# Attention and expert kernel: projection pieces cut in halves, one inverse square root for two norms, a new order of writes on the SyncE queue

## The chip, the cores and the metric

The kernel runs on one core of one Trainium2 chip. A core has TensorE (matrix products), VectorE, ScalarE, GpSimd, and SyncE, which here only issues DMAs. The metric is device microseconds of one execution. Everything that is not an output lives in on-chip SBUF, in the PSUM banks that TensorE writes, or in scratch tensors in DRAM.

## The reference

x and ctx are (8, 256, 512): batch, channel or row, time. Without the set-up code the reference is:

```
ln(x)   = (x - mean) / sqrt(var + 1e-5)               # over the last axis
q, k, v = Wq ln(x) + bq, Wk ctx + bk, Wv ctx + bv     # 1x1 projections, 256 channels
p       = softmax(q^T k / 4) per head                 # 16 heads of 16 channels, 512 x 512 scores
x1      = x + Wo (p v) + bo
z       = ln(x1)
h       = z * rsqrt(mean(z * z) + 1e-6) * rms_weight
top 2 of 8 experts by h router_w; moe = sum of weight * (silu(h Wg_e) * (h Wu_e)) Wd_e
out     = x1 + moe + (silu(h Sg) * (h Su)) Sd
```

All in float32. The second norm is a layer norm followed at once by an RMS norm of the same rows.

## The kernel before

The attention runs in 16 **slots** s = 0 to 15 (HALVES), one for half the heads of one batch: slot s works on batch s // 2. A slot has 32 **units** u, one for a tile of 128 keys by 512 queries of one head. The loop on each engine walks u in steps of two (ScalarE in steps of one) in program order, so the order is written out by hand, and semaphores join the engines.

TensorE does in each step of two units (loop at L903): the scores of both units (L850, into three PSUM banks st_ps), the max-pass products of two units of a later slot (L816, into three banks front_ps; the pass runs up to two slots ahead), and in every second step the products of four probability tiles with V (L863). ScalarE turns scores into probabilities (L725). VectorE reduces the max pass to row maxima (L963). When a slot's maxima are complete, TensorE turns them (turn_max, L835, at unit 12), VectorE copies them into a high and a low part (max_parts, L971 and L973, at unit 14), SyncE writes them out as rows (rows_out, L511) and reads them back under the Q stack (rows_in, L519), where the next slot's scores need them.

Between these, **projection pieces** run in one PSUM bank, proj_ps, which is handed from piece to piece. Slot s projects K and Q for slot s + 3, K at unit 2 and Q at unit 6 (KQ_UNITS, L246; project_qk, L779). At units 18 and 26 (late_units, L254) an even slot projects V for the next batch (project_v, L803), an odd slot the output projection of batch (s - 3) / 2 (project_out, L345). A piece is six matmuls of 512 columns or twelve of 256, since each product is made as high x high + high x low + low x high. ScalarE empties K and Q with their bias (qk_bias, L678) and V (v_copy) two units after the piece; VectorE adds the output projection to x (residual, L415, two units after) and takes its row statistics (L1006, four units after).

GpSimd has one list per slot (L633): the high and low part of K (L580, L584), the same of Q; in even slots then the load of C two batches ahead (L641), normalize (L594), the split of x (L600, L602) and the split of C (L614, L616); in odd slots split_attn (L607, L609), the split of the attention output for the output projection; then in both the division by the softmax sums (L410). project_out waits for split_attn by the semaphore attn_split, at its first matmul. In split_attn:

```
pool.wait_ge(attn_ready, ATTN_START + 2 * (b + 1))
pool.wait_ge(low_ready, 2 * min(2 * b + 7, HALVES))
```

SyncE's queue (L537) does per slot, in this order: numerators and denominators of the slot before out and back in, K parts out (write_part, L490), the K stack in (load_stack, L504), Q parts out, the maxima's rows out, the inverted denominators out (rec_out), the rows in, the inverted denominators in (rec_in), the Q stack in.

The norms need 1 / sqrt on VectorE without ScalarE's tables: a bit trick and three Newton steps, eleven small chained operations (row_rstd). row_scale does it twice, once for the layer norm and once for the RMS norm: in slot 14 for batches 0 to 5 (in three lumps at units 0, 4 and 8), and after the attention for batch 6 and for batch 7. In slot 3 one chain at unit 16 makes the input norm of batches 4 to 7. After the attention come the shared expert, the routing and 39 blocks of 128 rows through the experts; the change does not touch them.

Of the kernel before, what the change touches and what calls it, by code (L numbers as in the profile page):

```python
# [53 lines left out]
def xattn_ffn_kernel(nc, x, ctxt, wqkv_t, wo_t, bias_cols, rms_w, router_t, gate_up, down,  # L54
# [15 lines left out]
    with ExitStack() as outer:  # L70
# [15 lines left out]
        rstd2 = sb("rstd2", [P, B * CT])  # L86
# [103 lines left out]
        var_ready = sem("var_ready")  # L190
# [98 lines left out]
        count = {"step": 0, "var": 0}  # L289
# [75 lines left out]
        def row_variance(dve, lo, hi):  # L365
# [5 lines left out]
        def row_rstd(dve, lo, hi, dst, done=None):  # L371

            count["var"] += 1
            dve.wait_ge(var_ready, count["var"])
# [3 lines left out]
                                                 ALU.mult, ALU.add))  # L378
            for i in range(NEWTON):
                chained(dve, nc.vector.tensor_tensor(rs_c[:, lo:hi], rs_b[:, lo:hi], rs_b[:, lo:hi], ALU.mult))  # L380
                chained(dve, nc.vector.scalar_tensor_tensor(out=rs_c[:, lo:hi], in0=rs_c[:, lo:hi], scalar=-0.5, in1=rs_a[:, lo:hi],
                                                            op0=ALU.mult, op1=ALU.mult))
                last = nc.vector.scalar_tensor_tensor(out=(rs_b if i < NEWTON - 1 else dst)[:, lo:hi], in0=rs_c[:, lo:hi], scalar=1.5,
                                                      in1=rs_b[:, lo:hi], op0=ALU.add, op1=ALU.mult)
                if i < NEWTON - 1 or done is None:
                    chained(dve, last)
                else:
                    last.then_inc(done, 1)

        def row_scale(dve, lo, hi, steps=(0, 1, 2)):  # L390
            if 0 in steps:
                row_variance(dve, lo, hi)
            if 1 in steps:
                row_rstd(dve, lo, hi, rstd)
                chained(dve, nc.vector.tensor_tensor(rs_a[:, lo:hi], mv[:, lo:hi, 1], rstd[:, lo:hi], ALU.mult))
                chained(dve, nc.vector.tensor_tensor(rs_a[:, lo:hi], rs_a[:, lo:hi], rstd[:, lo:hi], ALU.mult))
                nc.vector.tensor_scalar(rs_a[:, lo:hi], rs_a[:, lo:hi], RMS_EPS, None, ALU.add).then_inc(var_ready, 1)
            if 2 in steps:
                row_rstd(dve, lo, hi, rstd2)
                chained(dve, nc.vector.tensor_tensor(rstd[:, lo:hi], rstd[:, lo:hi], rstd2[:, lo:hi], ALU.mult))  # L400
# [71 lines left out]
        with nc.Block() as block:  # L472

            @block.sync
            def _(sp):
# [61 lines left out]
                for s in range(HALVES):  # L537
# [26 lines left out]
            def _(pool):  # L564
# [68 lines left out]
                for s in range(HALVES):  # L633
                    if s + 3 < HALVES:
# [3 lines left out]
                    b = (s + 4) // 2  # L638
                    if s % 2 == 0 and b < B:
                        pool.wait_ge(v_ready, 2 * (b - 1))  # L640
                        nc.gpsimd.dma_start(c_sb[:, b % 2, :, :], c_t[b]).then_inc(c_loaded[b % 2], 16)  # L641
                        normalize(b)
                        split_xn(b)
                        split_c(b)
# [26 lines left out]
            def _(act):  # L671
# [46 lines left out]
                for s in range(HALVES):  # L718
                    proj = s + 3 < HALVES
                    for u in range(UNITS):  # L720
# [10 lines left out]
                        if proj and u - 2 in KQ_UNITS:  # L731
                            qk_bias(s + 3, KQ_UNITS.index(u - 2))
                        if value_batch(s) is not None and u - 2 in late_units(s):
                            v_copy(value_batch(s), late_units(s).index(u - 2))
# [3 lines left out]
            def _(pe):  # L738
# [9 lines left out]
                def project_qk(n, i, kts=range(CT)):  # L748
# [35 lines left out]
                def project_v(b, r):  # L784

                    if r == 1:
                        pe.wait_ge(vt_copied, 2 * b + 1)
                    elif b < 2:
                        pe.wait_ge(qk32_ready, 4 * (b + 1))
                    else:  # L790
                        pe.wait_ge(nm_parts_ready, turns(2 * b - 1))
                    for i in range(2):
# [12 lines left out]
                    mm.then_inc(v_ready, 1)  # L805
# [850 lines left out]
```

## Time and profile before

| | |
|---|---|
| median of 3 runs | 850.28 us (850.21 to 852.99) |
| profiled execution | 849.69 us, its span 847.9 us |
| TensorE busy | 803.9 us, 95% |
| VectorE busy | 518.1 us, 61% |
| ScalarE busy | 401.1 us, 47% |
| GpSimd busy | 353.1 us, 42% |
| attention slots | from about 54 to 516 us |

Busy time is what an engine's instructions cover. Matmuls overlap in the pipeline and their ends are modelled, so a TensorE shown as busy may still wait for a moment; start to start is the better measure of a matmul. A timeline row gives the start, the length, the engine and line, and in square brackets the idle time before it and what ended it.

### The profile page before, as it was taken

The page shows a single profiled execution, that of the slowest core. Times are in us where ns is not written, and L with a number is a line of the kernel's source. Part 1 is how long each engine was busy: PE and PEld are TensorE (multiplying, and loading weights), DVE is VectorE, ACT ScalarE, POOL GpSimd, SP SyncE. Part 2 cuts the span into 40 slices and gives each one's busy share as a digit, 9 for nine tenths or more (in the row PEclk, how much of TensorE's full clock was granted, in tenths as well). Part 3 has the DMA queues.
Part 4 walks back from the last instruction along what each step waited for, and adds up shares of the span by engine and source line. Part 5 has one row for each costly group of instructions (what it writes and reads, how often), then busy time and mean ns, then how long its engine had stood idle before and what let it go on. Part 6 is the DMA issues. An engine that isn't in the chain of part 4 may idle for free. (4 is left out here: it accounts for less than half of the span.)

```text
span 847.9 us, 11463 instructions
## 1 busy us (share of the span) xinstructions
PE 803.9 (95%) x3771; PEld 388.6 (46%) x3771; DVE 518.1 (61%) x1043; ACT 401.1 (47%) x751; POOL 353.1 (42%) x288
## 2 busy tenths in 40 slices
PE   6999999999999999999999998999999999999993
PEld 2434434444444444444433454443555555555552
DVE  5787888787777877878788655568542222222221
ACT  1115666767677677676776663110422323333231
POOL 4207417326354274253220211000117777777774
PEclk9999999999999999999999999999999999999998
DMA  8957557646665566466633223931626555655553
GB/s 275 211 95 224 114 127 166 132 103 141 145 137 129 119 157 149 103 149 143 131 80 106 91 77 110 415 111 51 251 56 99 98 97 97 101 90 96 95 98 43
DMA packets 54956, 110.48 MB, mean 130 GB/s; under 512 B 12580, under 2 KB 27684, under 8 KB 50660
## 3 DMA queue, kind: packets, MB, share of 16 engines
q1 hardware_dynamic: 37852, 80.23, 37.5%
q0 software_dynamic: 16960, 29.37, 18.4%
q8 instruction: 32, 0.52, 0.3%
q10 hardware_dynamic: 88, 0.16, 0.1%
q14 instruction: 24, 0.20, 0.1%
HBM read 68.44 MB, written 41.16 MB: 129 GB/s over the span
## 5 line engine op out<-in xcount | busy, mean ns | idle before, releaser
L963 DVE TENSOR_REDUCE negmax<-front_ps 128x1 f32<-128x512 f32 x512 | 323.6, 681 | 85.9 <-PE front_ps L816 85.5
L725 ACT ACTIVATE probs<-st_ps 128x512 f32<-128x512 f32 x512 | 280.2, 601 | 166.6 <-PE st_ps L850 149.9
L1215 POOL DMA_INDIRECT out<-x_sb,row_i x78 | 122.0, 1564 | 70.3 <-ACT x_sb L1263 57.0
L1408 PE MATMUL big_ps<-w_gu,attn 128*128 x312 | 140.4, 593 | 0.8 <-ACT attn L1255 0.8
L1602 DVE TENSOR_TENSOR zeros<-attn,big_ps 128x256 f32<-128x256 f32 x39 | 16.4, 421 | 116.3 <-ACT attn L1275 116.3
L850 PE MATMUL st_ps<-stacks 50*128 50x512 f32 x256 | 77.7, 488 | 5.4 <-ACT probs L725 4.3
L1408 PEld LDWEIGHTS big_ps<-w_gu,attn 128*128 128x128 f32 x312 | 56.2, 190 | 57.0 <-issue 57.0
L410 POOL TENSOR_TENSOR attn<-attn,recip 128x512 f32<-128x512 f32 x15 | 19.2, 1278 | 150.1 <-DMA recip<-rec_dram 150.1
L850 PE MATMUL st_ps<-q_stack,k_stack 50*128 50x512 f32 x256 | 74.6, 491 | 3.9 <-ACT probs L725 2.8
L580 POOL CAST early<-early 128x512 fp32r<-128x512 f32 x28 | 17.1, 610 | 136.4 <-ACT early L678 136.4
L816 PE MATMUL front_ps<-stacks 48*128 48x512 f32 x256 | 68.7, 434 | 3.8 <-DVE negmax L963 3.0
L1275 ACT ACTIVATE attn<-big_ps 128x256 f32<-128x256 f32 x39 | 15.0, 384 | 117.7 <-PE big_ps L1408 117.7
L816 PE MATMUL front_ps<-k_stack,q_stack 48*128 48x512 f32 x256 | 69.2, 425 | 0.8 <-DVE negmax L963 0.3
L863 PE MATMUL pv_ps<-probs,v_t 128*32 128x512 f32 x512 | 68.2, 605 | 0.5 <-ACT probs L725 0.5
L863 PE MATMUL pv_ps<-probs,early 128*32 128x512 f32 x512 | 68.2, 605 | 0.3
L850 PEld LDWEIGHTS st_ps<-stacks 50*128 50x128 f32 x256 | 29.6, 183 | 82.8 <-ACT probs L725 71.4
L1199 POOL DMA_INDIRECT x_sb<-h_rows,row_i x39 | 39.5, 1013 | 61.0 <-DVE row_i L1576 49.4
L850 PEld LDWEIGHTS st_ps<-q_stack,k_stack 50*128 50x128 f32 x256 | 28.4, 183 | 77.0 <-ACT probs L725 67.0
L1377 PE MATMUL big_ps<-down_high,act_parts 128*128 x156 | 59.1, 419 | 1.1 <-DVE act_parts L1594 1.1
L1291 PE MATMUL big_ps<-early,sh_gu 128*128 128x512 f32 x128 | 56.3, 594 | 0.0
L584 POOL TENSOR_TENSOR early<-early 128x512 fp32r<-128x512 f32 x32 | 41.0, 1281 | 12.3 <-DVE early L955 10.0
L1592 DVE CAST act_parts<-big_ps 128x256 fp32r<-128x256 f32 x39 | 16.5, 424 | 46.7 <-PE big_ps L1386 46.7
(199 smaller groups left out, 1056.6 us busy)
## 6 DMA issues: line engine op xcount, KB each, us to landing
parts_dram<-early SPq DMA_DIRECT2D x32, 512.0 KB, 6.2
stacks<-parts_dram SPq DMA_DIRECT2D x32, 256.0 KB, 5.6
w_gu<-in_gate_up SPq DMA_DIRECT2D x8, 1024.0 KB, 13.4
x_sb<-in_x SPq DMA_DIRECT2D x8, 512.0 KB, 9.9
early<-in_ctx POOLq DMA_DIRECT2D x8, 512.0 KB, 7.1
stacks<-parts_dram SPq DMA_DIRECT2D x32, 128.0 KB, 5.9
k_stack<-parts_dram SPq DMA_DIRECT2D x16, 256.0 KB, 5.1
q_stack<-parts_dram SPq DMA_DIRECT2D x16, 256.0 KB, 5.6
```

The costliest lines, as they stand in the source:

```text
L410: eng.tensor_tensor(half, half, recip[:, :], ALU.mult).then_inc(attn_ready, 1)
L584: nc.gpsimd.tensor_tensor(parts[:, i, 1, :], qk32[:, i, :], parts[:, i, 0, :].bitcast(F32), ALU.subtract).then_inc(low_ready, 1)
L725: nc.scalar.activation(probs[:, k % 2, u % GH, :], score_bank(UNITS * s + u), ACT.Exp, scale=SCALE).then_inc(exp_done, 1)
L816: nc.tensor.matmul(smax_bank(i), q_stack[buf][low:low + SROWS, pair, tt * P:(tt + 1) * P], k_stack[buf][low:low + SROWS, pair, :], start=T ...
L850: nc.tensor.matmul(score_bank(i), k_stack[buf][low:end, pair, st * P:(st + 1) * P], q_stack[buf][low:end, pair, :], start=True, stop=True, ...
L863: mm = nc.tensor.matmul(pv_ps[32 * j:32 * j + 32, :], v_t[n % NBUF][:, st, GH * g + j, :], probs[:, k % 2, j, :], start=(st == 0), stop=(s ...
L963: nc.vector.tensor_reduce(negmax[:, n % 2, c:c + 1], smax_bank(UNITS * n + u), AX_X, ALU.max, negate=True).then_inc(max_done, 1)
L1199: nc.gpsimd.indirect_dma_start(h_in[:, k % RING, :], None, h_rows, bass.IndirectOffsetOnAxis(ap=row_i[:, k:k + 1], axis=0)).then_inc(in_lo ...
L1215: nc.gpsimd.indirect_dma_start(outs[i], bass.IndirectOffsetOnAxis(ap=row_i[:, k:k + 1], axis=0), y_sb[:, k % RING, DY * i:DY * (i + 1)], N ...
L1291: mm = nc.tensor.matmul(big_ps[:, 2 * (j % 2) + i, :], sh_gu[:, a, i * F + c * P:i * F + (c + 1) * P], ht_all[:, g, a, :], start=(a == 0), ...
L1377: mm = nc.tensor.matmul(y_ps[:, k % 2, :], act[:, a, :], w[:, bass.ds(expert, 1), a, :], start=(a == 0 and i == 0), stop=(a == FT - 1 and ...
L1408: mm = nc.tensor.matmul(gu_ps[:, :], h_t[:, k % 2, a, :], w_gu[:, bass.ds(expert, 1), a, :], start=(a == 0), stop=(a == DT - 1))
```

## The change

In slots 3 to 12 (`spread`) each projection piece is done in two halves of three matmuls (V: six) four units apart: K at units 2 and 6, Q at 10 and 14, V or output at 18 and 22, and 26 and 30. A piece is emptied two units after its second half, that is K at unit 8, Q at 16, the third at 24, the fourth at unit 0 of the next slot. The turn of the maxima moves from unit 12 to unit 8, its copies from unit 14 to unit 8. VectorE takes the row statistics directly behind the residual. On SyncE the K stack's load moves behind the rows out, and the Q parts' write behind the rows in. On GpSimd the load of C moves to the head of the list and the split of C before the normalization, in all even slots. The norm after the attention becomes one inverse square root of var * (1 + 1e-6) + 1e-11, which is the product of the two; its steps in slot 14, and those of slot 3, are spread over units. project_out also waits for qk32_ready.

The core of the diff (left out: the count of the variance semaphore, renamed callers, the unchanged bodies of the Newton steps):

```diff
-        KQ_UNITS = (2, 6)
+        def spread(s):
+            return 3 <= s < HALVES - 3
         def turn_unit(s):
-            return 16 if s == 0 else 12
+            return 16 if s == 0 else 8 if spread(s) else 12
+        def parts_unit(s):
+            return turn_unit(s) if spread(s) else turn_unit(s) + 2
+        def kq_units(s):
+            return ((2, 6), (10, 14)) if spread(s) else ((2, 2), (6, 6))
         def late_units(s):
-            return (10, 14) if s == 0 else (18, 26)
+            return ((18, 22), (26, 30)) if spread(s) else ((10, 10), (14, 14)) if s == 0 else ((18, 18), (26, 26))
+        def halves_at(pieces, u):
+            for i, units in enumerate(pieces):
+                if u in units:
+                    return i, [j for j, unit in enumerate(units) if unit == u]
+            return None, []
+        def ended_at(pieces, u):
+            ends = [units[1] for units in pieces]
+            return ends.index(u - 2) if u - 2 in ends else None
...
         def project_out(pe, b, o, kt, bank):
                 pe.wait_ge(nm_parts_ready, turns(min(2 * b + 4, HALVES - 1)))
+                pe.wait_ge(qk32_ready, 2 * min(2 * b + 7, HALVES))
...
-            nc.vector.tensor_scalar(rs_a[:, lo:hi], mv[:, lo:hi, 1], LN_EPS, None, ALU.add).then_inc(var_ready, 1)
+            chained(dve, nc.vector.tensor_scalar(rs_a[:, lo:hi], mv[:, lo:hi, 1], scale, eps, ALU.mult, ALU.add))
-        def row_scale(dve, lo, hi, steps=(0, 1, 2)):
...
+        def token_variance(dve, lo, hi):
+            row_variance(dve, lo, hi, 1.0 + RMS_EPS, LN_EPS * RMS_EPS)
+        def token_scale(dve, lo, hi):
+            token_variance(dve, lo, hi)
+            row_rstd(dve, lo, hi)
...  SyncE
                     if proj:
                         write_part(s + 3, 0)
-                        load_stack(s + 3, 0)
-                        write_part(s + 3, 1)
+                        if not spread(s):
+                            load_stack(s + 3, 0)
+                            write_part(s + 3, 1)
                     if s + 1 < HALVES:
                         rows_out(s + 1)
+                    if proj and spread(s):
+                        load_stack(s + 3, 0)
                     if s > 0:
                         rec_out(sp, s - 1)
                     if s + 1 < HALVES:
                         rows_in(s + 1)
+                    if proj and spread(s):
+                        write_part(s + 3, 1)
                     if s > 0:
                         rec_in(sp, s - 1)
...  GpSimd
+                    b = (s + 4) // 2
+                    if s % 2 == 0 and b < B:
+                        pool.wait_ge(v_ready, 2 * (b - 1))
+                        nc.gpsimd.dma_start(c_sb[:, b % 2, :, :], c_t[b]).then_inc(c_loaded[b % 2], 16)
                     if s + 3 < HALVES:
                         for i in range(2):
                             high(s + 3, i)
                             low(s + 3, i)
                     if s % 2 == 0 and b < B:
+                        split_c(b)
                         normalize(b)
                         split_xn(b)
-                        split_c(b)
...  TensorE
                     elif 0 in kts:
                         pe.wait_ge(xn_ready, n // 2 + 1)
+                        if spread(s):
+                            pe.wait_ge(nm_parts_ready, turns(s + 1))
                 def turn_max(n):
-                    pe.wait_ge(qk32_ready, 2 * min(n + 3, HALVES))
+                    pe.wait_ge(qk32_ready, min(2 * n + 5, 2 * HALVES) if spread(n - 1) else 2 * min(n + 3, HALVES))
...
-                        if out_batch(s) is not None and u in late_units(s):
-                            for kt in range(CT):
-                                project_out(pe, out_batch(s), late_units(s).index(u), kt, proj_ps[:, :])
+                        if out_batch(s) is not None:
+                            for kt in parts_here:
+                                project_out(pe, out_batch(s), i, kt, proj_ps[:, :])
...  VectorE
                         if s == 3 and u == 16:
-                            row_rstd(dve, 4 * CT, B * CT, rstd, scale_ready)
+                            rstd_guess(dve, 4 * CT, B * CT)
+                        if s == 3 and u in (20, 22, 24):
+                            rstd_step(dve, 4 * CT, B * CT, (u - 20) // 2, scale_ready if u == 24 else None)
+                        if u == 0 and spread(s - 1) and out_batch(s - 1) is not None:
+                            residual(dve, out_batch(s - 1), 1, proj_ps[:, :])
+                            row_stats_of(out_batch(s - 1), 1)
-                        if u == turn_unit(s) + 2 and s + 1 < HALVES:
+                        if u == parts_unit(s) and s + 1 < HALVES:
                             max_parts(s + 2, UNITS)
...
-                            row_scale(dve, 0, EARLY, (u // 4,))
+                            token_variance(dve, 0, EARLY)
+                        if s == HALVES - 2 and u == 2:
+                            rstd_guess(dve, 0, EARLY)
+                        if s == HALVES - 2 and u in (4, 6, 8):
+                            rstd_step(dve, 0, EARLY, (u - 4) // 2)
...
-                row_scale(dve, EARLY, LAST)
+                token_scale(dve, EARLY, LAST)
```

## Rows read from the trace of the kernel before

**Rows 1.** Page, parts 1, 2, 5: busy us (share) xcount; tenths; busy, mean ns | idle.
```profile
PE 803.9 (95%) x3771; PEld 388.6 (46%) x3771; DVE 518.1 (61%) x1043; ACT 401.1 (47%) x751; POOL 353.1 (42%) x288
...
PEclk9999999999999999999999999999999999999998
...
L963 DVE TENSOR_REDUCE negmax<-front_ps 128x1 f32<-128x512 f32 x512 | 323.6, 681 | 85.9 <-PE front_ps L816 85.5
```

**Rows 2.** TensorE's timeline, slots 3 to 5: start us, length us, line, out<-in, count [idle before].
```profile
152.04 0.50 PE L779 MATMUL proj_ps<-c_high,w_high 128*128 128x512 f32 x1
...
182.06 0.50 PE L779 MATMUL proj_ps<-c_high,w_high 128*128 128x512 f32 x1
...
183.64 0.50 PE L850 MATMUL st_ps<-stacks 50*128 50x512 f32 x2
183.98 0.40 PE L816 MATMUL front_ps<-stacks 48*128 48x512 f32 x2
184.31 1.07 PE L863 MATMUL pv_ps<-probs,early 128*32 128x512 f32 x8
185.31 0.50 PE L850 MATMUL st_ps<-stacks 50*128 50x512 f32 x2
...
185.97 0.50 PE L779 MATMUL proj_ps<-xn_high,w_high 128*128 128x512 f32 x1
186.31 0.40 PE L779 MATMUL proj_ps<-down_high,w_high 128*128 128x512 f32 x1
186.54 0.39 PE L779 MATMUL proj_ps<-xn_high,w_low 128*128 128x512 f32 x1
...
187.56 0.50 PE L850 MATMUL st_ps<-stacks 50*128 50x512 f32 x2
...
188.22 1.06 PE L863 MATMUL pv_ps<-probs,early 128*32 128x512 f32 x8
...
191.16 1.06 PE L863 MATMUL pv_ps<-probs,early 128*32 128x512 f32 x8
...
209.75 0.50 PE L779 MATMUL proj_ps<-c_high,w_high 128*128 128x512 f32 x1
```

**Rows 3.** ScalarE's timeline: the Q bias in slots 4 and 5.
```profile
188.58 0.68 ACT L678 ACTIVATE early<-proj_ps,bias 128x512 f32<-128x512 f32 x1
...
216.27 0.68 ACT L678 ACTIVATE early<-proj_ps,bias 128x512 f32<-128x512 f32 x1
```

**Rows 4.** VectorE's timeline, slot 5: residual and row statistics.
```profile
227.27 0.74 DVE L415 SCALAR_TENSOR_TENSOR x_sb<-proj_ps,bo_all,x_sb 128x512 f32<-128x512 f32 x1
...
229.12 0.68 DVE L1006 BATCH_NORM_STATS2 stats<-x_sb 128x6 f32<-128x512 f32 x1
```

**Rows 5.** TensorE's timeline: output projection of slot 5, K piece of slot 6.
```profile
223.70 0.50 PE L345 MATMUL proj_ps<-down_high,w_o_high 128*128 128x512 f32 x1
...
238.06 0.50 PE L779 MATMUL proj_ps<-c_high,w_high 128*128 128x512 f32 x1
```

**Rows 6.** GpSimd's timeline, slot 5: second instruction of the attention split.
```profile
220.23 2.38 POOL L609 TENSOR_TENSOR attn_low<-attn,down_high 128x1024 fp32r<-128x1024 f32 x1
```

**Rows 7.** TensorE's timeline, slot 3, beside VectorE's square-root chain.
```profile
169.62 0.50 PE L816 MATMUL front_ps<-stacks 48*128 48x512 f32 x1 [0.53 <-DVE negmax L963]
```

**Rows 8.** SyncE's queue, slot 4: last issue of the Q stack.
```profile
205.30 0.42 SPq L506 DMA_DIRECT2D q_stack<-parts_dram  x1
```

**Rows 9.** TensorE's timeline, slot 14.
```profile
471.23 1.10 PE L746 MATMUL proj_ps<-zeros 128*128 128x512 f32 x2 [0.79 <-DVE nm_parts L973]
```

**Rows 10.** Timeline after the attention: VectorE's last step for batch 7, TensorE's turn.
```profile
546.09 0.16 DVE L400 TENSOR_TENSOR rstd<-rstd 128x2 f32<-128x2 f32 x1
...
548.79 0.44 PE L444 MATMUL front_ps<-ident,rows_or_down 128*128 128x128 f32 x2 [0.53 <-DVE rows_or_down L427]
```

**Rows 11.** TensorE's last matmul, and a stretch: busy us of each engine, PEclk, DMA.
```profile
835.31 0.40 PE L1377 MATMUL big_ps<-down_high,act_parts 128*128 x1
...
840.00:841.00 1.00, 0.00 (x0) 0.00 (x0) 0.00 (x0) 0.00 (x0) 0.70 (x2) 0.87 0.00 0
```

More of the change, by code:

```diff
@@ L288, in xattn_ffn_kernel @@
         EARLY = LAST - CT
-        count = {"step": 0, "var": 0}
+        count = {"step": 0}
         def out_batch(s):
@@ L378, in row_rstd @@
                                                  ALU.mult, ALU.add))
-            for i in range(NEWTON):
[L380 to L388, printed above, removed]
@@ L390, in row_scale, with rstd_step @@
-        def row_scale(dve, lo, hi, steps=(0, 1, 2)):
[L391 to L400, printed above, removed]
+        def rstd_step(dve, lo, hi, i, done=None):
+            chained(dve, nc.vector.tensor_tensor(rs_c[:, lo:hi], rs_b[:, lo:hi], rs_b[:, lo:hi], ALU.mult))
+            chained(dve, nc.vector.scalar_tensor_tensor(out=rs_c[:, lo:hi], in0=rs_c[:, lo:hi], scalar=-0.5, in1=rs_a[:, lo:hi],
+                                                        op0=ALU.mult, op1=ALU.mult))
+            last = nc.vector.scalar_tensor_tensor(out=(rs_b if i < NEWTON - 1 else rstd)[:, lo:hi], in0=rs_c[:, lo:hi], scalar=1.5,
+                                                  in1=rs_b[:, lo:hi], op0=ALU.add, op1=ALU.mult)
+            if done is None:
+                chained(dve, last)
+            else:
+                last.then_inc(done, 1)
@@ L730, in _ @@
                             pv_copy(2 * s)
[L731 to L734, printed above, removed]
+                        if u == 0 and spread(s - 1) and value_batch(s - 1) is not None:
+                            v_copy(value_batch(s - 1), 1)
+                        if proj and ended_at(kq_units(s), u) is not None:
+                            qk_bias(s + 3, ended_at(kq_units(s), u))
+                        if value_batch(s) is not None and ended_at(late_units(s), u) is not None:
+                            v_copy(value_batch(s), ended_at(late_units(s), u))
                 pv_copy(2 * HALVES - 1)
@@ L782, in project_qk, with project_v @@
                         mm.then_inc(qk_ready, 1)
[L784 to L792, printed above, removed]
+                def project_v(b, r, tiles=(0, 1)):
+                    if 0 in tiles:
+                        if r == 1:
+                            pe.wait_ge(vt_copied, 2 * b + 1)
+                        else:
+                            pe.wait_ge(qk32_ready, 4 * (b + 1))
+                            if b >= 2:
+                                pe.wait_ge(nm_parts_ready, turns(2 * b - 1))
+                    for i in tiles:
                         st = 2 * r + i
@@ L804, in project_v @@
                                                           start=(kt == 0 and j == 0), stop=(kt == CT - 1 and j == PRODUCTS - 1))
-                    mm.then_inc(v_ready, 1)
+                    if 1 in tiles:
+                        mm.then_inc(v_ready, 1)
                 def max_pass(n, u):
@@ L911, in _ @@
                             pv(STEPS * s + u // GH - 1)
-                        if s + 3 < HALVES and u in KQ_UNITS:
-                            project_qk(s + 3, KQ_UNITS.index(u))
+                        i, kts = halves_at(kq_units(s), u)
+                        if s + 3 < HALVES and kts:
+                            project_qk(s + 3, i, kts)
                         if u == turn_unit(s) and s + 1 < HALVES:
                             turn_max(s + 1)
-                        if value_batch(s) is not None and u in late_units(s):
-                            project_v(value_batch(s), late_units(s).index(u))
-                        if out_batch(s) is not None and u in late_units(s):
-                            for kt in range(CT):
-                                project_out(pe, out_batch(s), late_units(s).index(u), kt, proj_ps[:, :])
+                        i, parts_here = halves_at(late_units(s), u)
+                        if value_batch(s) is not None and parts_here:
+                            project_v(value_batch(s), i, parts_here)
+                        if out_batch(s) is not None:
+                            for kt in parts_here:
+                                project_out(pe, out_batch(s), i, kt, proj_ps[:, :])
                         if s == 0 and u == 0:
```

29 lines of the change are left out of this document (12 added, 17 removed).

## The prediction

> **What bounds the kernel now.** I read the page first. TensorE is busy for 95% of the span, at the full granted clock of 2.4 GHz [rows 1], so a gain must come out of TensorE's own sequence and not out of another engine's load. "Busy" hides short waits, because the ends of matmuls are modelled, so the second view is TensorE's timeline of slot 4. Its steps are regular [rows 2]: a pair of score matmuls 0.34 us (183.64 to 183.98), a pair of max-pass matmuls 0.33, the eight products with V 1.00 (184.31 to 185.31). A group of four units from one V product to the next is V product, scores, maxima, piece, scores, maxima. With a six-matmul projection piece it takes 188.22 - 184.31 = 3.91 us, without one 191.16 - 188.22 = 2.94 us. The work of the second is only 1.00 + 2 x (0.34 + 0.33) = 2.34 us, so 0.60 us of each group without a piece is spent on the round trip through VectorE's maxima and ScalarE's exponentials. Slot 4 has four groups of each sort: 4 x (3.91 + 2.94) = 27.4, and the turn of the maxima adds 0.2. The K pieces of slots 4 and 5 start 27.69 us apart (182.06, 209.75) [rows 2], which agrees.
>
> **Halves in slots 3 to 12: the gain.** The piece takes 1.59 us (185.97 to 187.56). Its first matmul costs 0.34, the next 0.23 each, the last 0.33 with the change back to the scores [rows 2]. Half a piece, three matmuls, is 0.34 + 0.23 + 0.33 = 0.90. Every group of four units now holds one half: 3.91 - (1.59 - 0.90) = 3.22 us, above the 2.94 of the round trip, so that wait vanishes behind real work. Two groups take 6.44 instead of 6.85: 0.41 saved per piece, four pieces a slot, **1.6 us**. Bounds: at least 0.8, if a switch to a half piece and back costs twice what I read (0.2 more per piece); at most 4 x (6.85 - 2 x 2.94) = 3.9, if half a piece vanished wholly in the round trip's 0.60. I take 1.6, which is the reading itself, for K, Q, V and output pieces alike, since each is six matmuls of 512 columns or twelve of 256.
>
> Against it stand tighter hand-overs. The turn now follows the V product of unit 8 directly. The K bias on ScalarE starts 1.02 us after the scores of its unit (187.56 to 188.58) and takes 0.68 [rows 2, 3]; TensorE wants the bank at 0.34 + 0.33 + 1.00 = 1.67, so it waits about 0.1. The two copies of the turned maxima must then end before the Q piece of unit 10: another 0.1. So a slot without an output piece goes from 27.7 to 27.7 - 1.6 + 0.2 = 26.3 us: **-1.4**, five times (slots 4, 6, 8, 10, 12): -7.0.
>
> In odd slots VectorE's residual (0.74 us) and row statistics (0.68) [rows 4] now stand one behind the other, and the next piece reuses the bank only two units later. The pair's maxima end about 2.05 us after its scores (0.34, 0.40 for the first product, two reductions of 0.68 that overlap a little [rows 1]), the residual at 2.75; TensorE is there at 2.34: 0.45 us of wait, twice per odd slot. Odd slots show 238.06 - 209.75 = 28.31 us now [rows 2, 5]; without what follows they would be 26.3 + 0.9 = 27.2: -1.1. Bounds of the 0.9: from 0.6, what they lose to the same work now (28.3 - 27.7), to 1.5.
>
> **The wait that the change creates.** GpSimd runs its list in order. In an odd slot it is: high and low part of K, high and low part of Q, then the split of the attention output into its high and low part, then the division. That order is not edited. But the bias of Q, on which the Q parts wait, moves from unit 8 to unit 16, and the output projection, which needs the split (attn_split), stays at unit 18. Now: Q's bias starts at 216.27 [rows 3], the second instruction of the split starts at 220.23 and lasts 2.38 [rows 6], so the split is there 222.61 - 216.27 = 6.34 us after the bias started. The projection starts at 223.70 [rows 5], 1.1 us after that: no wait today. After the change the bias starts 1.02 us after the scores of unit 16, the split is ready at 1.02 + 6.34 + 0.06 = 7.4 us, and TensorE stands at the projection after 0.34 + 0.33 + 1.00 + 0.34 + 0.33 = 2.34 us. **It waits 5.1 us**, in slots 3, 5, 7, 9 and 11. Behind the waiting matmul are all later scores, maxima and V products; ScalarE and VectorE run empty, and nothing gives the time back, since every group after it is bound by TensorE. Bounds: not under 3.5 (if ScalarE's bias came 1.6 us ahead of its place, which in-order exponentials exclude), not above 7 (if GpSimd's steps stretched by a third). An odd slot then takes 27.2 + 5.1 = 32.3 instead of 28.3: **+4.0**, four times (5, 7, 9, 11): +16.0. Slot 3 takes 182.06 - 152.04 = 30.02 us now, since eleven chained square-root steps on VectorE make TensorE wait there, 0.53 us in one row [rows 2, 7]; spread out they cost some 0.2, so slot 3 comes to 32.5: +2.5.
>
> **Other edges.** In even slots GpSimd gets Q at about 15 us, splits C until 20.8, normalizes, splits x until 28.5, 2 us into the next slot; the first user, Q's piece at unit 10, comes 8 us into it, C's at unit 2: nothing lost. On SP the Q parts are written only after the maxima's rows; each queue step behind them counts. Today the last load of the Q stack is issued at 205.30 [rows 8], 25.6 us after the slot's first scores (2.3 before 182.06), and its first user is unit 8 of the next slot, 35.6 us after them. In the new order the bias of Q is done at 15 us, its parts at 17, SP writes them at 18.3 once the maxima's rows are through, waits for the inverted rows until about 22.5 and issues the last load near 24.5; the user comes at 26.3 + 6.8 = 33.1. So 8.6 us of cover where there are 10.0 today. I cost it at nothing; if the landing takes longer, slots 5, 7, 9 and 11 pay what is missing, up to 2 us each. C's load moves to the head of GpSimd's list, away from the stack loads, and is used 15 us later: nothing. The new wait for qk32_ready in the output projection is met whenever attn_split is: nothing.
>
> One inverse square root for both norms: in slot 14 TensorE's 0.79 us wait for the copies of the maxima [rows 9] goes, since VectorE no longer runs a second chain of twelve steps ahead of them: -0.8 (0 to -1.5). For batch 6 at the end of attention, VectorE waits for the denominators' DMA anyway: nothing. For batch 7 the chain ends in 546.09 + 0.16 today; fifteen steps of 0.2 go [rows 10], and TensorE's wait of 0.53 before the turn at 548.79 [rows 10] vanishes, the rest being under its own gates: -0.5 (0 to -3).
>
> **The sum.** -7.0 + 16.0 + 2.5 - 0.8 - 0.5 = +10.2 on the profiled execution of 849.69 us (span 847.9 and 1.8 around it): 859.9. The median of the three runs stands 0.6 higher at 850.28, so 860.5 us.
>
> **Rivals.**
> *The clock falls in the new waits.* TensorE stands still for 5.0 us each time. At the end of this trace its last matmul ends at 835.7 and the granted clock of 840 to 841 us is 0.87, of which 0.26 us at the half level: it fell 5.0 us after the last matmul [rows 11], from 2.4 to 1.2 GHz. For it: the same length of rest. Against it: gaps up to 2.1 us in this trace left it at 1.00. If it falls, the matmuls behind each wait run at half speed for a while; between half a group (+1.6 us) and a whole one (+3.2): +8 to +16, so 868.5 to 876.5, nearer the first.
> The Trainium skill, "TensorE: Matmul & The Clock Gate", Part 1, says that the clock is halved after the array has been idle and given back only after it has been busy again for some time; by that rule this rival is the forecast, by the forecast's sum it is not; the row at the end of the trace agrees with the rule and can't tell whether 5.0 us are enough in mid-kernel.
>
> *The stacks come late.* The Q stack of the next slot lands after unit 8 of odd slots: +1 to +2 in four slots, 864.5 to 868.5. For it: the cover shrinks by 1.4 us. Against it: odd slots are longer by the wait itself.
>
> *No wait at unit 18: faster.* If the split is done before TensorE reaches unit 18, the gains stand alone: five even slots -7.0, four odd -4.4, slot 3 at 27.4 instead of 30.0 -2.6, -1.3 elsewhere: -15.3, so 835 us. It would take a TensorE that arrives later (bound by VectorE or ScalarE) or a split that runs ahead of Q's parts. The break is at a wait of 15.3 / 5 = 3.1 us instead of 5.1: below it the change is no loss. For it: the halves fill idle time as computed. Against it: GpSimd's order and four measured durations.
>
> **Numbers.** Forecast 0.62 (own range 855 to 865), clock 0.18, stacks 0.06, faster 0.14 (0.01 of it so near to nothing that it counts as no change). About 0.5% is what a measurement of this kernel tells from no change. Slower by over 0.5%: 0.83; within: 0.04; faster: 0.13. The range 853 to 874 leaves out the faster case and the far end of the clock's.
>
> **What would show it.** Odd slots of 32 us and even ones of 26.3; in TensorE's waits five of about 5 us at the output projection, released by GpSimd's second split instruction; no wait there in even slots; groups of 3.22 us without the 2.94 ones; granted clock below 1 behind the waits only if the first rival holds. If the five waits are absent the forecast is wrong by its main step and the time is near 835; if they are there but the slots between are not shorter, the halves' step failed.

## The result, and the profile after

Over six runs each the changed kernel takes 884.44 us (879.41 to 886.27) and the kernel before 850.50 (849.69 to 852.99): ratio 1.038, 95% interval 1.036 to 1.040. The forecast was 860.5 with a range from 853 to 874: slower as forecast, but by 34 us and not by 10. The profiled run took 884.68 us, its span is 882.9, 35.0 more than before.

The same parts of the page after (busy us, share, xcount; tenths of the clock; busy, mean ns | idle):

```profile
PE 812.1 (92%) x3771; PEld 380.8 (43%) x3771; DVE 519.6 (59%) x998; ACT 405.2 (46%) x751; POOL 353.0 (40%) x288
...
PEclk9999999899799899899699999999999999999998
...
L1001 DVE TENSOR_REDUCE negmax<-front_ps 128x1 f32<-128x512 f32 x512 | 326.7, 685 | 111.9 <-PE front_ps L852 110.1
```

Beside [rows 1] the number of matmuls is the same and TensorE's busy time is 8.2 us longer. The clock's line says why: it was 9 in every slice but the last, and now has dips from slice 8 to slice 20, which is the attention. VectorE's maxima are as long as before.

The waits of TensorE after (who waited on whom: us in total, times, longest; some rows left out):

```profile
PE proj_ps L367 <- POOL attn_low L638: 25.2, 5, 5.1
PE front_ps L852 <- DVE negmax L1001: 4.0, 7, 0.8
PE proj_ps L813 <- DVE x_sb L439: 3.4, 5, 0.7
...
PE proj_ps L813 <- DVE nm_parts L1011: 2.1, 10, 0.2
PE proj_ps L367 <- DVE x_sb L439: 1.9, 3, 1.2
```

The first is the forecast wait: five times 5.1 us (4.93 in slot 3, 5.06 in the others) at the output projection, released by the second split instruction. The rows on x_sb (at the K piece) and on nm_parts are hand-overs that the forecast put at 0.45 and 0.1 us each: 0.7 and 0.2.

One odd slot (11) after. TensorE's timeline, which answers to [rows 5]:

```profile
374.56 0.47 PE L813 MATMUL proj_ps<-c_high,w_high 128*128 128x512 f32 x1 [0.68 <-DVE x_sb L439]
...
400.96 0.50 PE L813 MATMUL proj_ps<-c_high,w_high 128*128 128x512 f32 x1
...
414.10 0.40 PE L852 MATMUL front_ps<-stacks 48*128 48x512 f32 x2
419.56 0.77 PE L367 MATMUL proj_ps<-down_high,w_o_high 128*128 128x512 f32 x1 [5.06 <-POOL attn_low L638]
420.13 0.63 PE L367 MATMUL proj_ps<-attn_low,w_o_high 128*128 128x512 f32 x1
420.55 0.63 PE L367 MATMUL proj_ps<-down_high,w_o_low 128*128 128x512 f32 x1
421.12 0.80 PE L886 MATMUL st_ps<-q_stack,k_stack 50*128 50x512 f32 x2
421.71 0.63 PE L852 MATMUL front_ps<-stacks 48*128 48x512 f32 x2
422.27 1.93 PE L899 MATMUL pv_ps<-probs,v_t 128*32 128x512 f32 x8
424.13 0.79 PE L886 MATMUL st_ps<-q_stack,k_stack 50*128 50x512 f32 x2
...
437.38 1.07 PE L899 MATMUL pv_ps<-probs,v_t 128*32 128x512 f32 x8
...
439.82 0.47 PE L813 MATMUL proj_ps<-c_high,w_high 128*128 128x512 f32 x1 [0.71 <-DVE x_sb L439]
```

ScalarE's Q bias and GpSimd's list in the same slot (answering to [rows 3] and [rows 6]):

```profile
413.12 0.68 ACT L708 ACTIVATE early<-proj_ps,bias 128x512 f32<-128x512 f32 x1
```

```profile
413.87 0.61 POOL L609 CAST early<-early 128x512 fp32r<-128x512 f32 x1 [5.05 <-ACT early L708]
414.56 1.27 POOL L613 TENSOR_TENSOR early<-early 128x512 fp32r<-128x512 f32 x1
415.96 1.04 POOL L636 CAST down_high<-attn 128x1024 fp32r<-128x1024 f32 x1
417.08 2.34 POOL L638 TENSOR_TENSOR attn_low<-attn,down_high 128x1024 fp32r<-128x1024 f32 x1
```

And the same stretch cut into windows (us, busy us and count of PE, PEld, DVE, ACT, POOL, granted clock as a share of 2.4 GHz, DMA share, GB/s):

```profile
414.50:417.00 2.50, 0.00 (x1) 0.00 (x0) 1.29 (x2) 1.37 (x3) 2.30 (x2) 1.00 0.97 153
417.00:419.50 2.50, 0.00 (x0) 0.00 (x0) 0.00 (x0) 0.00 (x0) 2.34 (x1) 0.61 0.87 222
419.50:434.00 14.50, 14.44 (x49) 5.61 (x53) 6.65 (x11) 4.91 (x10) 1.27 (x1) 0.50 0.42 73
434.00:439.00 5.00, 5.00 (x31) 1.54 (x23) 3.96 (x7) 2.78 (x7) 0.00 (x0) 0.94 0.00 0
```

Q's bias starts at 413.12. The split is ready at 417.08 + 2.34 = 419.42, 6.30 us later (forecast 6.34). GpSimd's first instruction, Q's high part, had itself waited 5.05 us for that bias. Before the wait is over, at about 417.6, the clock falls from 2.4 to 1.2 GHz. It stays at 1.2 through 14.5 us in which TensorE is busy for 14.44, and comes back at about 435. Eight products with V take 422.27 to 424.13 = 1.86 us where they took 1.00 [rows 2]. So this odd slot lasts 439.82 - 400.96 = 38.86 us instead of 28.3. The even one ahead of it lasts 400.96 - 374.56 = 26.40, where 27.69 stood before and 26.3 was forecast.

I read the clock in 1-us windows over the whole span. Before it never left 1.00 in the attention. After, it is at 1.2 GHz there in seven stretches, 54.6 us in all: one at each of the five waits (6.8, 10.2, 6.8, 6.8 and 17.1 us long), one at 182 to 186, and one at 485 to 490 (3.4 us each), the last in slot 13, where there is no long rest. Each of the five begins inside its wait, 2.9 to 4.4 us after TensorE stopped. So the forecast wait is there, and a cost that the sum did not have lies on top.

### The profile page after: what moved, and what is told of

Read it like the earlier page. It is cut to its first block and busy times, and to the rows that moved or that the text cites. A ratio compares the mean times of both kernels' runs of the same rounds, so it can differ in the third digit from the quotient of the medians.

```text
span 882.9 us, 11450 instructions
## 1 busy us (share of the span) xinstructions
PE 812.1 (92%) x3771; PEld 380.8 (43%) x3771; DVE 519.6 (59%) x998; ACT 405.2 (46%) x751; POOL 353.0 (40%) x288
## 5 line engine op out<-in xcount | busy, mean ns | idle before, releaser
L755 ACT ACTIVATE probs<-st_ps 128x512 f32<-128x512 f32 x512 | 284.3, 598 | 197.0 <-PE st_ps L886 180.3
L609 POOL CAST early<-early 128x512 fp32r<-128x512 f32 x28 | 17.1, 611 | 227.0 <-ACT early L708 227.0
L899 PE MATMUL pv_ps<-probs,v_t 128*32 128x512 f32 x512 | 72.7, 642 | 0.5 <-ACT probs L755 0.5
L886 PE MATMUL st_ps<-stacks 50*128 50x512 f32 x256 | 69.8, 504 | 2.2 <-ACT probs L755 2.0
L899 PE MATMUL pv_ps<-probs,early 128*32 128x512 f32 x512 | 70.4, 623 | 0.3 <-ACT probs L755 0.2
L886 PE MATMUL st_ps<-q_stack,k_stack 50*128 50x512 f32 x256 | 68.9, 516 | 0.8 <-ACT probs L755 0.7
L852 PE MATMUL front_ps<-stacks 48*128 48x512 f32 x256 | 59.6, 430 | 2.9 <-DVE negmax L1001 2.2
L852 PE MATMUL front_ps<-k_stack,q_stack 48*128 48x512 f32 x256 | 60.2, 417 | 2.1 <-DVE negmax L1001 1.8
L886 PEld LDWEIGHTS st_ps<-stacks 50*128 50x128 f32 x256 | 26.3, 187 | 77.7 <-ACT probs L755 61.6
L886 PEld LDWEIGHTS st_ps<-q_stack,k_stack 50*128 50x128 f32 x256 | 25.8, 190 | 75.4 <-ACT probs L755 58.3
```

The lines of the kernel that those rows point to most:

```text
L755: nc.scalar.activation(probs[:, k % 2, u % GH, :], score_bank(UNITS * s + u), ACT.Exp, scale=SCALE).then_inc(exp_done, 1)
L852: nc.tensor.matmul(smax_bank(i), q_stack[buf][low:low + SROWS, pair, tt * P:(tt + 1) * P], k_stack[buf][low:low + SROWS, pair, :], start=T ...
L886: nc.tensor.matmul(score_bank(i), k_stack[buf][low:end, pair, st * P:(st + 1) * P], q_stack[buf][low:end, pair, :], start=True, stop=True, ...
L899: mm = nc.tensor.matmul(pv_ps[32 * j:32 * j + 32, :], v_t[n % NBUF][:, st, GH * g + j, :], probs[:, k % 2, j, :], start=(st == 0), stop=(s ...
```

## The experiments

The theory after the result (A): the 35.0 us are the wait (25.2), the clock behind it (about 18), and a gain of the halves that is smaller than forecast (about -8 instead of -15). Rivals: that the clock costs little and the halves themselves cost time; that the clock falls whatever the length of the rest; that the new order of SyncE's queue holds the stacks back.

### The split ahead of Q's parts

attn_high shares its memory with qk32, the tile into which the projected K and Q are emptied (both start at element 3072 of the same buffer). That is why the split waits for Q's low part, the last reader of qk32; a change of order alone would overwrite K and Q. Here it has 4 KB per partition of its own, shared in time with data that is reloaded in slot 14, and the split heads GpSimd's list:

```
+ attn_high = sb("attn_high", [P, 2, T], F32R)
...
- pool.wait_ge(low_ready, 2 * min(2 * b + 7, HALVES))
+ pool.wait_ge(bo_ready, 1)
+ pool.wait_ge(wo_split, 1)
+ if b > 0: pool.wait_ge(y_ready, CT * b)
...
  for s in range(HALVES):
+     if out_batch(s) is not None and out_batch(s) < B - 2:
+         split_attn(out_batch(s))
      if s + 3 < HALVES: ...
-     (the same two lines behind Q's and K's parts)
```

> The changed kernel with its split of the attention output moved from behind Q's high and low part to the head of GpSimd's list in odd slots. For that the split's high half gets a place of its own (that of w_o and rms_w, which are loaded again in slot 14), since its old place is the one of the K and Q tile. Theory (the wait at unit 18 and the clock that falls behind it are the whole loss): the five waits of 5.1 us go, the granted clock stays at 1.00 through slots 3 to 12, even slots stay at 26.4 us, odd ones come to 27.2 to 27.8, and the time to 835 to 840 us. Rival (the halves themselves, with their many short waits, bring the clock down or cost more than they save): the waits go, but stretches at the half clock remain, odd slots stay above 30 and the time is 855 to 862.

Measured 843.44 us (841.52 to 844.12), 0.992 of before (0.9905 to 0.9935), span of the profiled run 839.8. That is 3 us above my theory's 835 to 840 and far below the rival's 855. The five waits are gone and in the profiled run, the fastest, the clock is 1.00 all through the attention. The other three runs have a mean clock of 0.989 to 0.992 where it has 0.995, so they were at 1.2 GHz for some more microseconds; no trace shows where. Slot 11 now ends like this, and TensorE's waits at the projections from 152 to 440 are:

```profile
397.53 0.40 PE L861 MATMUL front_ps<-stacks 48*128 48x512 f32 x2
...
398.59 0.47 PE L822 MATMUL proj_ps<-c_high,w_high 128*128 128x512 f32 x1 [0.66 <-DVE x_sb L442]
```

```profile
PE proj_ps L822 <- DVE x_sb L442: 3.3, 5, 0.7
PE proj_ps L368 <- DVE x_sb L442: 2.6, 5, 1.1
PE proj_ps L822 <- DVE nm_parts L1020: 2.1, 10, 0.2
```

The order of GpSimd's list is the whole loss: the other parts of the change gain 847.9 - 839.8 = 8.1 us of span (6.9 by the medians, 850.38 - 843.44). Slots 3 to 11 last (before; here; changed kernel):

```
slot           3     4     5     6     7     8     9    10    11
before       30.02 27.69 28.31 27.70 28.32 27.74 28.32 27.69 28.33
split ahead  29.80 26.41 27.78 26.41 27.74 26.42 27.72 26.41 27.73
changed      37.44 26.41 36.55 26.40 34.91 26.42 34.96 26.40 38.86
```

The changed kernel's odd slots exceed these by 7.2 to 11.1 us, of which 5.1 is the wait: 2.1 to 6.1 each is left, which theory A puts down to the clock. The control, the same memory and list order put into the kernel before, where the split is ready in time anyway:

> The kernel before with the split's own place for its high half (w_o and rms_w loaded again in slot 14) and the split at the head of GpSimd's list, whole pieces, old queue order. It is the control for split_ahead: every theory expects no change, 849.5 to 851.5, as the split was not waited for; what split_ahead gains against the kernel before is then the halves' and not the new place's. If the new place or the two loads matter, it shows here.

850.63 us, 0.9998 (0.9988 to 1.0007): nothing, as expected. The 8 us do not come from the split's own memory.

### The same wait with the clock held up

Zero matmuls into the output projection's bank, ahead of its wait for the split, fill part of the rest. Five of them:

```
+ if spread(2 * b + 3):
+     for _ in range(5):
+         nc.tensor.matmul(bank, zeros[:, 0:P], zeros[:, :], start=True, stop=True)
  pe.wait_ge(attn_split, b + 1)
```

The run with four:

> The changed kernel, and ahead of the wait for the split in odd slots 3 to 11 TensorE multiplies zeros four times (128x512 float32, 1.06 us each) into the bank that it is about to use. The wait stays: GpSimd's chain is untouched. Theory (a stretch of rest of about 5 us lets the clock fall, and that is all that my sum lacked): TensorE's own waits at the output projection shrink to 0.5 to 1 us each, the granted clock stays at 1.00, odd slots take 32 to 33 us, and the time is 859 to 865, near what was forecast. Rival (the long odd slots come from something else behind the wait, such as ScalarE or VectorE refilling the pipeline, or late stacks): 878 to 886, odd slots stay at 35 to 38.

870.48 us, ratio 1.023 (1.022 to 1.025): extra work on TensorE makes the changed kernel 14 us faster. That is between my theory's 859 to 865 and the rival's 878 to 886. The waits for the split are still 1.2 to 1.35 us each, since a product of zeros took 0.93 us and not 1.06, and 13.7 us are left at 1.2 GHz: 3.4 in slot 7, 6.8 in slots 13 and 14, 3.4 just behind the attention. Slots 5, 9 and 11 take 32.80 to 32.81 (27.74 + 5.06), and slot 7 takes 34.36, where the clock fell behind a rest of 1.35. Then five:

> As fill_four with five products of zeros, 5.3 us: TensorE has no rest left ahead of the split. Theory (the loss is additive: the wait's 5 x 5.1 us and the clock): split_ahead's 843.4 + 25.5 + 5 x 0.2 = 870 us or a little less, odd slots 32.8 to 33.1, no half clock in slots 3 to 12. Rival (half clock is not about the rests at the wait): falls in slots 3 to 12 as many as in fill_four, and 872 to 878.

873.08 us (868.89 to 878.25), 1.029 (1.025 to 1.032): by its median where the rival put it, and 3 us above what I expected. Only the fastest of the four runs has a trace. In it slots 3 to 11 are all at 2.4 GHz, against the rival. They sum to 271.7 us and the changed kernel's to 288.4: **the clock costs 16.7 us there**. The 271.7 are split ahead's 246.4 plus 5 x 5.05. But 6.8 us of slots 13 and 14, which are as in the changed kernel, are at 1.2 GHz, behind waits of 0.74 us on VectorE, and so are 3.4 us just behind the attention. The other three runs have lower mean clocks (0.977 to 0.986, here 0.988), and no trace shows where theirs fell. The cleaner test is the last experiment below. Three:

> As fill_four with three products of zeros ahead of the wait: TensorE's rest there is 1.3 + 1.06 = 2.4 us instead of 1.3 (no fall behind it) or 3.5 in split_between (a fall behind all five). Theory A (what counts is the single rest, and 2.4 us is nearer to 1.3): no half clock behind the waits, 868 to 872 as fill_four. Theory B (2.4 us with the thin work around it is enough): half clock behind some of the five, 873 to 882.

874.97 us, 1.028 (1.024 to 1.031): theory B. With rests of 2.1 to 2.2 us there is half clock behind four of the five waits and none behind the other (slot 5, 32.80 us), 27.3 us in all. The longest stretch is 13.7 us, behind a rest of 2.20 in slot 7.

### A shorter rest without extra work

As split ahead, but in slots 3 to 11 the split stands between Q's high and low part:

```
  high(s + 3, i)
+ if i == 1 and splits and spread(s): split_attn(out_batch(s))
  low(s + 3, i)
```

> As split_ahead, but in odd slots 3 to 11 the split stands between Q's high and low part on GpSimd's list: a wait of 1.02 + 0.68 + 0.06 + 0.69 + 3.5 - 2.34 = about 3.6 us less the overlap, say 3.0 to 3.7 us at unit 18 instead of 5.1. Theory (the clock falls only behind the long rest): no half clock, odd slots 30.5 to 31.5, time 852 to 857. Rival (any rest of 3 us brings it down too): stretches at the half clock behind most waits, time 865 to 875.

873.88 us, 1.022 (1.020 to 1.024), with single runs up to 886. The rival held: five times 3.4 to 3.5 us, and 1.2 GHz at every one of them (13.6 and four times 10.2 us). TensorE's waits, and the clock around the end of the one from 413.2 to 416.7:

```profile
PE proj_ps L368 <- POOL attn_low L647: 17.5, 5, 3.5
```

```profile
415.00:416.00 1.00, 0.00 (x0) 0.00 (x0) 0.00 (x0) 0.00 (x0) 1.00 (x1) 0.99 0.56 53
416.00:427.00 11.00, 10.32 (x38) 3.86 (x38) 4.36 (x7) 3.26 (x6) 3.04 (x3) 0.54 0.59 146
```

By the traces, the waits are 25.2 - 17.5 = 7.7 us shorter than after, but slots 3 to 11 only 6.2 (282.2 against 288.4), with at least as much half clock (64.8 us in all, where after has 54.6). The median is 10.6 us lower. So by the traces a shorter rest gave back no more than its own length: 3.5 us bring the clock down as well as 5.1.

### The norms alone

The kernel before with one inverse square root for both norms, its steps spread over units (in short, not the code itself):

```
- rs_a = mv + LN_EPS; rstd; rs_a = mv*rstd*rstd + RMS_EPS; rstd2; rstd * rstd2
+ rs_a = mv * (1 + RMS_EPS) + LN_EPS * RMS_EPS; guess at u = 2; steps at u = 4, 6, 8
```

> The kernel before with only the change of the norms: one inverse square root for both norms after the attention, its steps and those of slot 3 spread over units. Forecast's step: slot 3 from 30.0 to about 28.5, TensorE's 0.79 us wait in slot 14 gone, 0.5 after the attention: 847 to 848 against 850.3. Rival (VectorE's chains are hidden by other waits): 849.5 to 850.5, slot 3 stays at 30.

850.76 us, 0.9999 (0.9986 to 1.0012): nothing, as the rival had it. Slot 3 lasted 31.89 us (30.02 before), longer and not 1.5 us shorter. The half clock below can account for up to 1.7 of the 1.9; that the steps spread over units still delay maxima that TensorE waits for is my reading of the rest. The clock halved for 3.4 us with no long rest near it, only waits of 0.21, 0.63 and 0.22 us in the 4 us ahead (TensorE's timeline, and a window inside):

```profile
172.72 0.50 PE L816 MATMUL front_ps<-stacks 48*128 48x512 f32 x1 [0.63 <-DVE negmax L963]
...
175.11 0.60 PE L816 MATMUL front_ps<-stacks 48*128 48x512 f32 x1 [0.22 <-DVE negmax L963]
...
176.23 0.63 PE L343 MATMUL proj_ps<-attn_low,w_o_high 128*128 128x512 f32 x1
```

```profile
175.00:178.00 3.00, 2.89 (x7) 2.00 (x7) 2.93 (x7) 0.77 (x2) 1.28 (x1) 0.56 0.99 169
```

### SyncE's old order

Split ahead, but the K stack's load and the write of Q's parts stand ahead of the maxima's rows again, as in the kernel before (their later places, not shown, are taken out):

```
- if not spread(s):
-     load_stack(s + 3, 0)
-     write_part(s + 3, 1)
+ load_stack(s + 3, 0)
+ write_part(s + 3, 1)
```

> split_ahead with SyncE's queue in the order of the kernel before: K stack in and Q parts out ahead of the maxima's rows. Theory (the new order is needed, since Q's parts are ready only at about 17 us of a slot): the rows go out at 17.6 instead of 11, are back under the Q stack at 25 to 27 us, and the next slot's first scores, due at 26.4, wait 0 to 2 us in each of ten slots: 845 to 860. Rival (the rows land in time anyway): 842 to 845, no wait for rows_in at the scores.

844.16 us (841.91 to 846.21), 0.993 (0.990 to 0.996), beside 843.44: not told apart in time. I had expected 845 to 860; the rival held. The trace shows slot 7 at 29.02 us with a wait of 1.13 us for a stack at 268.40, where 27.74 stands with the new order. The spans of the two traces are 1.3 us apart (841.1 and 839.8), which is inside the scatter of either kernel; the forecast gave the new order nothing.

### VectorE's order: the missing part of the gain

If the gain is short because the maxima go ahead of the residual, the residual ahead of the maxima should bring it. Split ahead plus (in short):

```
  for u in range(0, UNITS, TILES):
+     residual(...)   # of u = 0 and of u, ahead of the unit's maxima
      while found < maxima_until(s, u): ...
-     residual(...)
-     row_stats_of(...)
+     row_stats_of(...)   # two units later
-     if s == 3 and u in (14, 16, 20, 22, 24):   # input norm's steps
+     if s == 4 and u in (4, 8, 12, 14, 18):
```

> split_ahead with three more edits on VectorE: the residual stands ahead of its unit's maxima instead of behind them, the row statistics two units after it as in the kernel before, and the square-root chain of the input norm is spread over slot 4 (no output piece there) instead of slot 3. Theory (odd slots stay 1.3 us above even ones because TensorE waits 0.7 us for the residual twice; slot 3 and slot 13 lose 2.0 and 1.3 us to VectorE work piled up behind one piece): odd slots 26.6 to 27.0, slot 3 near 27, slot 13 as before, 834 to 838 against 843.4. Rival (the maxima, now later by the residual's 0.74, become the wait): odd slots stay at 27.5 to 28, 841 to 844.

**833.24 us** (832.19 to 834.85), 0.980 (0.978 to 0.982): the best version, faster than both kernels. Odd and even slots are now 26.35 to 26.44, but for slot 4 (27.42), which has the norm's chain now, and slot 8 (27.20), where TensorE waits 0.60 us for the Q stack's DMA. Against split ahead, slots 5, 7, 9 and 11 give 5.5 us together, slot 3 gives 3.4, and slots 4 and 8 take 1.8 back. VectorE's residual, TensorE's next K piece, and the waits of TensorE:

```profile
389.96 0.74 DVE L442 SCALAR_TENSOR_TENSOR x_sb<-proj_ps,bo_all,x_sb 128x512 f32<-128x512 f32 x1
```

```profile
391.87 0.50 PE L822 MATMUL proj_ps<-c_high,w_high 128*128 128x512 f32 x1
```

```profile
PE proj_ps L822 <- DVE nm_parts L1020: 2.4, 10, 0.5
```

The residual ends at 390.70, over 1 us ahead of the piece that takes its bank, and no wait on x_sb is left. Last, VectorE's order is put into the changed kernel, with its wait for the split and five products of zeros in each wait. The forecast had summed just this: the wait, a clock that stays up, and halves that gain what was read:

> fill_five with the three edits of residual_ahead on VectorE: the wait for the split stays, TensorE's clock is kept up by zeros, VectorE's hand-overs are cured. Theory: the forecast's sum with its two missing terms taken out, 833.2 + 25.5 + 1 = 859 to 861 us, odd slots 31.8 to 32.2. Rival (VectorE's cure is worth less once TensorE waits anyway, because the wait lets VectorE catch up): 864 to 870.

858.36 us (856.53 to 858.92), 1.009 (1.007 to 1.011). No half clock before the end of the kernel; slots 5 to 11 are 31.43 and 26.44 us, so the wait costs 31.43 - 26.36 = 5.07. The medians say the same: 858.36 - 833.24 = 25.1 us for five waits. With the clock held up, then, a wait costs its own length and nothing else, although ScalarE and VectorE run empty in it as before.

## Why the prediction was wrong

**The wait: right.** Forecast 5.1 us in slots 3, 5, 7, 9 and 11; measured 5.06 in four of them and 4.93 in slot 3, 25.2 in all. Split ahead is the causal test: 35.0 + 8.1 = 43.1 us of span (41.0 by the medians) hang on the order of GpSimd's list alone.

**The step that failed: no term for the clock.** The sum stood at "+10.2" with TensorE at 2.4 GHz behind each wait, and the rival's case against was "gaps up to 2.1 us in this trace left it at 1.00". Those gaps lay at the start and behind the attention, and they say nothing of 5 us. The row that did [rows 11] I called a rival of 0.18. It has the clock fall 5.0 us after the last matmul, which left the case open; in the five waits it fell after 2.9 to 4.4 us. 25.2 of the 43.1 us are the wait; 16.7 are the clock in slots 3 to 11, by the slots of the filled kernel; the last 1.2 are of the size of the half-clock stretch in slot 13, by subtraction. The rival's own price, half a group to a whole one per wait (8 to 16, "nearer the first"), was low as well: the stretches of 6.8 to 17.1 us, of which 0.7 to 2.2 lie in the wait and cost nothing, cost 2.1 to 6.1 us each. Beside this term, the gain of all other parts was 8.1 us and not 15.3. The two add up: 10.2 forecast + 17.9 for the clock + 7.2 for the gain that is missing = 35.3, of 35.0 measured.

The Trainium skill, "TensorE: Matmul & The Clock Gate", Part 1, says that idleness halves the clock and that it takes a time of sustained work to come back. The traces agree: 0.50 behind every rest of 3.4 to 5.1 us, with 4.6 to 15.1 us of work in after before 1.00 is back.
The same part of the Trainium skill adds that how many matmuls run slow at a kernel's start varies from run to run. No run here shows that, as each kernel has one trace; inside one trace, stretches of 6.8 to 17.1 us stand at equal waits.

**The halves: mechanism right, size too large.** A group takes 3.23 us (forecast 3.22), even slots 26.4 (26.3), waits at the turn 0.2 (0.1). Odd slots came to 27.74, not 27.2. The two residual waits, forecast at 0.45 each, are 0.37 at the output projection and 0.7 at the K piece, so 1.1 and not 0.9; but an odd slot of split ahead is 27.74 - 26.41 = 1.33 longer than an even one, and no wait shows the last 0.3. The 1.33 is gone with the residual put first, so it is the residual's and its row statistics' in any case. That is 4 x 0.55 = 2.2 us. Slot 3 came to 29.8 and not 27.4: VectorE has spread steps, residual and maxima there, one instruction of the chain took 1.28 us, and TensorE waits 1.15 at the projection. The rows are split ahead's; the changed kernel has the same work in that slot, and its own waits there:

```profile
165.80 1.28 DVE L399 TENSOR_SCALAR rs_b<-rs_a 128x8 int32<-128x8 int32 x1
```

```profile
165.77 1.28 POOL L619 TENSOR_TENSOR early<-early 128x512 fp32r<-128x512 f32 x1
```

```profile
168.06 0.49 PE L861 MATMUL front_ps<-stacks 48*128 48x512 f32 x1 [0.67 <-DVE negmax L1010]
...
174.59 0.50 PE L368 MATMUL proj_ps<-attn_high,w_o_high 128*128 128x512 f32 x1 [1.15 <-DVE x_sb L442]
```

That is 2.4 more. The instruction of 1.28 us starts 0.03 after GpSimd's low part of Q and ends 0.03 after it. In the changed kernel the pair is the same (1.26 us, from 165.09 and 165.06). In the kernel before, in norms alone and with the residual ahead it met no such GpSimd instruction and took 0.15 to 0.16. So the later Q bias, which moved GpSimd's work onto VectorE's chain, seems to have cost VectorE 1.1 us here; no run was made to test it. Slot 13, which I gave nothing, lost 1.2 (eight units take 7.77 us in split ahead and 7.18 before, twice): row statistics stand directly behind the residual there, and TensorE waits 0.74 twice on the maxima. With VectorE's order mended the gains are what the rival "no wait" took: 833.24 measured, 835 forecast. With the wait put back and the clock held, 858.36 stands beside the forecast's 860.5.

**Slot 14 and the norms: over-estimated.** Spreading the chain in slot 3 was to save 1.5 us by itself; in norms alone the slot is 1.9 us longer, half clock included. The wait of 0.79 [rows 9] became 0.34 (a gain of 0.4, forecast 0.8). The wait of 0.53 before the turn [rows 10] is gone as forecast, but from the first turn of batch 7 to the end the kernel takes 301.3 us after and 300.3 before, so that nothing was gained (forecast -0.5). From slot 13 and 14, TensorE's timeline after:

```profile
484.12 0.49 PE L852 MATMUL front_ps<-k_stack,q_stack 48*128 48x512 f32 x1 [0.75 <-DVE negmax L1001]
...
486.47 0.79 PE L367 MATMUL proj_ps<-down_high,w_o_high 128*128 128x512 f32 x1
...
505.47 1.10 PE L778 MATMUL proj_ps<-zeros 128*128 128x512 f32 x2 [0.34 <-DVE nm_parts L1011]
```

The first two rows also show the clock's fall in slot 13: a wait of 0.75 us, and a projection matmul of 0.79 us behind it where [rows 5] has 0.50.

**Queue order and stacks: right.** The stacks [rows 8] came in time, and TensorE has no wait for them in the attention after. The cover is thin, though: once the slots were down to 26.4 us (residual ahead), one Q stack came 0.60 us late in slot 8.

**What stays open.** Why the half clock lasts 6.8 us at one wait and 17.1 at another of the same length, and why waits of 0.2 to 0.75 us suffice at 175 us (norms alone) and 485 us (after) while one of 1.15 at 174.59 in split ahead does not. No run separates the work before the wait from its length. Nor does a run separate the residual's place from the moved chain.

## What to carry to other kernels

When the emptying of a result is moved later, follow every item behind it on each in-order engine that handles it: here a bias moved by eight units pushed an unrelated split past its user. Price a rest of TensorE as the rest plus the clock: here 5.1 us cost 7 to 11. If the trace of before has a rest of that length and the clock falls in it, that row is the best evidence there is, wherever it stands; but where it fell there, after 5.0 us, was no bound for the waits here. On an engine with slack put first what frees a shared bank, then what has only its own reader: with the norm's chain moved out of slot 3, that was worth 10 us here by the medians, more than the 7 that the other parts gain without it.

## What the hardware showed that I had not expected

- The granted clock stayed at 1.2 GHz for 14.5 us in which TensorE was busy for 14.44. Half speed was not over as soon as work was back.
- It also fell without a long rest: behind waits of 0.21, 0.63 and 0.22 us (norms alone), 0.74 (filled with five) and 0.75 (changed kernel).
- The clock fell behind four of five rests of 2.2 us (one of them 2.07), behind one of five of 1.2 to 1.35, and at five of five of 3.4 to 3.5. In the kernel before it fell behind none, but there the longest inside slots 3 to 14 is 0.79 us; those of 1.8 and 2.1 us lie outside the attention.
- Five products of zeros in each of the five waits, which compute nothing, took 16.7 us out of slots 3 to 11.
- A VectorE instruction on 128x8 numbers took 1.26 and 1.28 us beside one of GpSimd that ran as long, and 0.15 to 0.16 without it.
